# A fused attention and sparse FFN layer on eight cores: the FFN's down projection moved ahead of the next gate/up product, one step deep instead of two

## The reference, cut to what matters

```python
D_MODEL = 2048; NHEAD = 16; I = 8192                  # x is (4, 4096, 2048), float32
x = x + layernorm(attn(layernorm(x)))                 # q, v, decayed scan, gate, output projection
x = x + layernorm(ffn(layernorm(x)))

def ffn(x):
    h = silu(x @ w_gate) * (x @ w_up)                 # (rows, 8192)
    g = h.reshape(B, S, I // 4, 4)                    # groups of four neighbours
    _, idx = top_k(abs(g), 2)                         # the two largest stay, the others become 0
    h_sparse = (g * mask(idx)).reshape(B, S, I)
    return h_sparse @ w_down
```

## Time and profile before

| | us |
|---|---|
| runs without a profile | 7206.3 and 7617.3, median 7411.8 |
| profiled execution, its own time | 7094.9 |
| its span on core 0, first to last instruction | 7093.3 |
| TensorE matmuls busy | 4395.0 (62% of the span) |
| VectorE busy | 2056.2 (29%) |
| ScalarE busy | 1001.5 (14%) |
| DMA, mean rate | 92 GB/s |

### The profile page before, as it was taken

How to read it: one execution, slowest core, us unless ns; L and a number is a source line. 1 busy time by engine, 2 the same in 40 slices (tenths; PEclk the granted TensorE clock), 3 DMA queues, 4 the chain that set the end, 5 groups by cost and what they waited for, 6 DMA issues and landing times.

```text
span 7093.3 us, 51305 instructions; the slowest of 8 cores (7029.1 to 7093.3 us)
## 1 busy us (share of the span) xinstructions
PE 4395.0 (62%) x19010; PEld 2042.4 (29%) x19374; DVE 2056.2 (29%) x2796; ACT 1001.5 (14%) x1033; POOL 166.9 (2%) x232
## 2 busy tenths in 40 slices
PE   0237888466436678578488488588488588343443
PEld 0013444234213333233233233233233233111111
DVE  1522323212224423223233233233223233222222
ACT  2301111111110111111111211111211111100000
POOL 0000000000000000000000000000000000000000
PEclk9998778778768889889799799799799799666776
DMA  5300000222443321423623522523533523422223
GB/s 158 136 3 30 30 33 30 84 83 78 150 148 125 121 75 57 164 68 66 176 51 69 166 56 66 166 57 73 159 63 80 151 60 91 143 80 80 71 68 95
DMA packets 140829, 649.30 MB, mean 92 GB/s; under 512 B 15652, under 2 KB 15652, under 8 KB 107812
## 3 DMA queue, kind: packets, MB, share of 16 engines
q1 hardware_dynamic: 110630, 461.44, 19.9%
q0 software_dynamic: 29952, 184.56, 11.7%
HBM read 453.00 MB, written 192.94 MB: 91 GB/s over the span
## 4 chain that ended last, share of the span: by engine, by line
PE 59%; DMA 18%; DVE 10%; ACT 7%; issue 5%; SPq 1%; DVEq 0%; ACTq 0%; POOL 0%; POOLq 0%
PE psB L694 15%; PE psA L738 13%; PE psA L735 13%; PE psB L358 9%; PE psA L358 5%; DMA stg<-w_up 3%; DMA bp<-s_xn3T 3%; PE psA L338 2%; ACT fp L747 2%; DMA s_acc<-wslotB 2%; ACT bp L758 2%; DMA stg<-w_down 1%; DMA fp<-s_acc 1%; DVE stats L312 1%; DMA stg<-Wo 1%
## 5 line engine op out<-in xcount | busy, mean ns | idle before, releaser
L735 PE MATMUL psA<-wslotA,bp 128*128 128x512 bf16 x3949 | 1535.5, 389 | 1010.2 <-DMA bp<-s_xn3T 990.8
L738 PE MATMUL psA<-wslotA,bp 128*128 128x512 bf16 x4096 | 1588.5, 388 | 7.7
L735 PEld LDWEIGHTS psA<-wslotA,bp 128*128 128x128 bf16 x4096 | 408.4, 100 | 1531.4 <-issue 1071.8
L738 PEld LDWEIGHTS psA<-wslotA,bp 128*128 128x128 bf16 x4096 | 407.8, 100 | 501.8 <-issue 39.8
L358 PE MATMUL psB<-wslotA,bp 128*128 128x512 bf16 x2002 | 502.6, 414 | 48.2 <-ACT bp L343 44.1
L358 PE MATMUL psA<-wslotB,bp 128*128 128x512 bf16 x1512 | 376.7, 413 | 206.5 <-DMA bp<-s_ygT 204.9
L694 PE MATMUL psB<-wslotB,l_mat 128*128 128x512 bf16 x1399 | 382.3, 438 | 141.2 <-DVE bp L772 90.7
L694 PE MATMUL psB<-wslotB,t_mat 128*128 128x512 bf16 x1430 | 388.1, 436 | 120.7 <-DVE bp L772 90.1
L702 DVE COPY wslotB<-psB 128x2048 f32<-128x2048 f32 x128 | 293.3, 2292 | 580.2 <-PE psB L694 580.2
L747 ACT ACTIVATE fp<-psA 128x1024 f32<-128x1024 f32 x128 | 131.1, 1024 | 2328.3 <-PE psA L738 2328.1
L694 PE MATMUL psB<-wslotB,fp 128*128 128x512 bf16 x1151 | 309.4, 432 | 98.8 <-DVE bp L772 71.1
(11 more groups left out here) (128 smaller groups left out, 3221.0 us busy)
## 6 DMA issues: line engine op xcount, KB each, us to landing
s_acc<-wslotB POOLq DMA_DIRECT2D x128, 1024.0 KB, 8.2
stg<-w_gate SPq DMA_DIRECT2D x128, 512.0 KB, 5.6
stg<-w_up SPq DMA_DIRECT2D x128, 512.0 KB, 5.9
bp<-s_xn3T SPq DMA_DIRECT2D x128, 512.0 KB, 3.3
stg<-w_down SPq DMA_DIRECT2D x128, 512.0 KB, 6.1
fp<-x SPq DMA_DIRECT2D x48, 1024.0 KB, 5.3
stg<-Wq SPq DMA_DIRECT2D x32, 512.0 KB, 4.7
stg<-Wv SPq DMA_DIRECT2D x32, 512.0 KB, 4.5
```

The costliest lines, as they stand in the source:

```text
L735: ins = tt.matmul(psA[:, n * 512:(n + 1) * 512], xT[:, kc, :], fgc[:, kc, n * 512:(n + 1) * 512], start=(kc == 0), stop=(kc == KC - 1))
L738: ins = tt.matmul(psA[:, 1024 + n * 512:1024 + (n + 1) * 512], xT[:, kc, :], fuc[:, kc, n * 512:(n + 1) * 512], start=(kc == 0), stop=(kc ...
```

## The change

In all blocks the pending depth is one: two `hbuf` buffers serve everywhere, and step t calls `drain(t-1)`. The call stands at another place: at the head of the step, right behind SP's load of `s_xn3T[t]` and ahead of GU(t), where it stood behind the chain of t. No operation is added or removed.

```diff
     def ffn():
-        hbuf = [p0buf[0].bitcast(F32), p0buf[1].bitcast(F32),
-                fpool[2][:][:, 0:ICW]]
-        hflats = [p0buf[0], p0buf[1], fpool[2][:].bitcast(BF16)[:, 0:2 * ICW]]
-        r_h = [r_p0b[0], r_p0b[1], r_fp[2]]
+        hbuf = [p0buf[0].bitcast(F32), p0buf[1].bitcast(F32)]
+        hflats = [p0buf[0], p0buf[1]]
+        r_h = [r_p0b[0], r_p0b[1]]
...
         def drain(pend):
             pt, pic = pend
-            par = ((pic * NT + pt) % 3) if pic < NIC - 1 else (pt % 2)
+            par = pt % 2
...
                      dma=True, reads=[r_sxn3T[t]], writes=[r_bp[bx]])
+                if pending:
+                    drain(pending.pop(0))
                 xT = bpool[bx][:].rearrange("p (a b) -> p a b", b=128)
...
-                hpar = ((ic * NT + t) % 3) if ic < NIC - 1 else (t % 2)
+                hpar = t % 2
...
-                maxp = 2 if ic < NIC - 1 else 1
-                if len(pending) >= maxp:
-                    drain(pending.pop(0))
                 pending.append((t, ic))
                 emit_w(2)
```

## The result

The changed kernel is slower. The ratio to the kernel before is 1.085, with a 95% interval from 1.080 to 1.091. Over all its runs the median is 7826.5 us (7669.0 to 8208.9, 11 runs), that of the kernel before 7169.5 (7050.4 to 7635.6, 10 runs).

A forecast was written before the change was run, and what follows sets the result against it. TensorE was taken to bound the middle steps, waiting for weights between blocks and for loads in block 8. From the profiled execution, 7094.9 + 919 - 223 = 7791, so 7790 us, 9.8% slower, range 7650 to 8050.

The forecast's parts named there:

- the two regimes: Blocks 1 to 7 and block 8, priced separately: +919 us for the seven blocks, -223 us for block 8.
- The open chain: Middle step: TR waits from silu's start to h(t), 9.61 us, plus 0.15 us handover; TR then takes 1.94 us.
- The cast: Middle step, between TR and DN: 1.78 us, where the kernel before had 2.74 us.
- DN: Middle step: DN takes 9.1 us after a long idle time, with bounds 8.1 and 9.9.
- the 2.0 us for the low start: Middle step: loss added to DN's 7.07 us because the clock starts low after a long idle time.
- A block: Each of blocks 1 to 7: 52.0 + 14 x 36.5 + 13.9 + 68.5 = 645.4 us, against 514.1.
- GU(0) to GU(1): Start of blocks 1 to 7: GU(1) starts 52.0 us behind GU(0), against 45.5 before.
- the end of GU(15) to the next GU(0): Ends of blocks 1 to 7: silu(15) to the next GU(0) falls from 81.1 to 68.5 us.
- Block 8: Last block with the program's end: steps of 47.7 us, 796.9 us in all against 1019.5, a gain of 223 us.
- That TensorE passes a waiting matmul: Rival: GU(t) starts while TR(t-1) waits, so a step keeps 27.4 us; 6900 us in all; chance 0.03.
- That it stays cold through DN: Rival: all 32 matmuls of DN run at 1.2 GHz, 13.7 us instead of 9.1; 8380 us in all; chance 0.05.
- That the clock stays up: Rival: despite the waits, 0.9 us less on TR and 2.0 less on DN; 7420 us in all; chance 0.06.

The follow-up runs named there:

- the short chain: Changed kernel without absolute value, seven min/max operations, comparison and mask product: 6689.6 and 6690.9 us; same edit on the kernel before: ratio 0.965.
- e1_head_two: Changed kernel with the drain still at the head of the step, but of the tile two steps earlier: 6782.3 to 6811.7 us, ratio 0.957.
- e4_blocks1to7_only: Kernel before with the drain's new place and depth one in blocks 1 to 7 only, three buffers kept: 7917.6 and 7922.9 us, ratio 1.122.
- e7_cast_ahead: Changed kernel draining the tile two steps earlier, with TR and its cast emitted right behind silu, before the absolute value: 6544.6 and 6547.9 us, ratio 0.926.
- e6_fill: Changed kernel with 40 more matmuls of 512 columns behind each GU, their result unread: 7551.2 us in a single execution.

## Why the prediction was right, point by point

The direction, the two regimes and the terms were right, and the range held the time; but 7672 us lies only 22 us above its lower end. The 118 us by which the forecast of 7790 is too high have two sources. One is the start: the execution of 7094.9 us was itself 35 us above 7060, and its core 0 began block 1 at 2475 us, most of its other cores at 2406 to 2424. The other is the sum. The forecast sum was +696 us on that execution. The parts as measured, 7 x (639.2 - 514.1) = +876 and 767.6 - 1019.5 = -252, give +624, and from 7060 us 7684, where 7669 to 7685 were measured. So the loss was overestimated by 72 us by these parts, 43 in the seven blocks and 29 in block 8, and by 84 us by the totals (+612). The last 12 us are within the spread of the cores: on core 7 of the kernel before a block takes 516.4 us, and with that the parts give +608.

- **The open chain**: 9.61 + 0.15 us expected, 9.84 measured. TR at 1.94 us: measured in every step. It is shown to be the chain by the short chain (the wait falls by 7.2 us) and to be the order by e1_head_two.
- **The cast**: 1.78 us expected, 1.30 measured. The row I took it from stood behind a cast after which DN waited another 0.6 us; in the changed kernel the cast ends 0.15 us ahead of DN.
- **DN**: 9.1 us expected; 8.4 to 10.0 measured, with a mean of 9.0 over blocks 1 to 7 of e4_blocks1to7_only, so the 2.0 us for the low start were right. The step came out as 36.05 us, not 36.5.
- **A block**: 645.4 expected, 639.2 measured. It is nearly all the step, 14 x 0.45 = 6.3 us. GU(0) to GU(1) was 51 to 54 us (52.0), the end of GU(15) to the next GU(0) 67 to 69 (68.5 from silu).
- **Block 8**: 796.9 expected, 767.6 measured, the term that was most off. A step is 45.8 us and not 47.7. The casts' 0.5 us are a part of that. The other is the stretch from the eviction's start to the end of LN: 26.0 us in the earlier trace rows, 24.5 in the step shown above. That is mostly the choice of the row: the statistics behind that eviction waited 15.0 us for `s_acc`, but over the sixteen tiles of block 8 they wait 14.5 us in the mean (13.9 to 15.2) in the kernel before, and 14.0 (13.3 to 16.0) in the changed one; 13.5 us in the step shown is a short one. So a mean over the block would have given some 0.5 us less per step than the row, and why the changed kernel waits another 0.5 us less is open.
- **The rivals.** That TensorE passes a waiting matmul: excluded, as TR's idle time stands there in full. That it stays cold through DN: DN would be 13.7 us, and no middle one took more than 10.0. That the clock stays up: DN would be 7.07 and TR 1.06, and none was.

What the prediction noted and didn't price is the 2.74 us between TR and DN in the kernel before. With the cast ahead of the absolute value the gap shrank by 1.0 us (2.4 to 1.4 in the mean) and DN by another 0.9 (8.7 to 7.8), 1.8 us on a middle step.

## What to carry to other kernels

When a consumer is moved nearer to its producer in the list of an engine that runs in order, the chain of other engines that ran beside an older tile's work stands open in full, at every step. The number of buffers tells nothing of this: three or two made no difference here, while the same drain one tile later turned +8.5% into -4%. These 4% come from the program's last block: there the drain holds a layernorm whose store stands in SP's list, and issuing the next tile's load ahead of it took 63 us steps to 46 and less. The place of a call is to be judged by every engine's list, each regime by itself. Where an in-order engine holds two operations, the one that the bounding engine waits for belongs first, and the gap that it leaves costs TensorE its clock besides.

## What the runs showed of the hardware

Waits of little over a microsecond are not free for TensorE's clock. With 1.38 and 1.41 us around a TR of 1.06 (e7_cast_ahead), about every second DN ran low near its start (granted clock 0.61 over the first 1.6 us of the one at 4617.10) and took 8.75 us, where 7.07 is the time at 2.4 GHz throughout (1.00 in the one at 4643.51). The waits are the same at both, so they alone don't decide it; what else does was not tried. At the ends of blocks 1 to 7 in the kernel before, TR follows a DN without idle time and DN follows after 1.74 us: 14 such DNs took 7.07 us each. Behind the 9.84 us of the changed kernel all of TR (1.94 us for 1.06) and the start of DN ran low. Forty matmuls that nobody needs, put into the wait, brought 1.9 us of some 2.8 back in each step (e6_fill).
